# Graph attention on one core: a finer wait for the gathers, and two operands of VectorE kept in PSUM

## What is computed

```python
h  = (x @ W).reshape(n, HEADS, OUT_C)            # 8 heads of 32 channels
a1 = jnp.sum(h * attn_l, axis=-1); a2 = jnp.sum(h * attn_r, axis=-1)
e  = leaky_relu(a1[src] + a2[dst], 0.2)
ex = jnp.exp(e - seg_max[dst])
denom   = segment_sum(ex, dst)
message = h[src] * (ex / denom[dst])[:, :, None]
out     = segment_sum(message, dst)
```

## Time and profile before

| | |
|---|---|
| median of 3 runs | 3406.3 us (3402.91 to 3411.7) |
| span of the profiled execution | 3357.5 us (the rest of a run, some 49 us, lies around it) |
| busy: PE / DVE / ACT / POOL | 71% / 50% / 18% / 55% of the span |
| gathers on POOL | 1712, mean 1057 ns |
| DMA traffic | 302 MB, mean 90 GB/s |

### The profile page before, as it was taken

One profiled execution on the slowest core, in us unless ns is written; L12 is line 12 of the kernel. 1 busy time (PEld: TensorE's weight loads), 2 busy tenths in 40 slices (PEclk: granted clock), 3 DMA queues, 4 the chain that ended last, 5 costly groups with the idle time before them and its releaser, 6 DMA issues.

```text
span 3357.5 us, 47799 instructions
## 1 busy us (share of the span) xinstructions
PE 2396.9 (71%) x13450; PEld 1756.6 (52%) x13451; DVE 1666.8 (50%) x3416; ACT 614.4 (18%) x1640; POOL 1856.6 (55%) x1764
## 2 busy tenths in 40 slices
PE   4666776766677767666767666676778765379998
PEld 2554455545555555554545445554555554347776
DVE  6544445544445454544545445454555554733334
ACT  2411111111111111111111111011111111043332
POOL 3366666666666666666666666666666676200000
PEclk9878887878788777877878778888888887789999
DMA  6533333333333333333333333333334333100000
GB/s 193 200 99 88 89 96 93 96 97 92 91 96 93 92 97 92 89 94 92 91 97 96 93 91 101 100 99 96 109 106 109 109 94 84 39 29 19 19 19 20
DMA packets 150658, 302.18 MB, mean 90 GB/s; under 512 B 36163, under 2 KB 88347, under 8 KB 150620
## 3 DMA queue, kind: packets, MB, share of 16 engines
q0 software_dynamic: 82848, 233.35, 25.9%
q1 hardware_dynamic: 66100, 66.77, 6.1%
q10 hardware_dynamic: 1672, 1.59, 0.2%
HBM read 269.29 MB, written 32.29 MB: 90 GB/s over the span
## 4 chain that ended last, share of the span: by engine, by line
PE 43%; another core or an unknown queue 22%; DVE 16%; issue 12%; DVEq 2%; ACT 2%; POOL 2%; DMA 0%; ACTq 0%; SPq 0%; POOLq 0%
PE bank L872 16%; PE bank L985 5%; DVE work L1264 4%; PE bank L881 4%; PE bank L824 4%; PE bank L975 4%; DVE acc L1271 3%; PE bank L890 2%; PE bank L836 2%; PE bank L879 2%; POOL work L548 2%; PE bank L785 1%; DVEq L1256 1%; DVE zb L1245 1%
## 5 line engine op out<-in xcount | busy, mean ns | idle before, releaser
L548 POOL DMA_INDIRECT work<-h_tab,idx x1712 | 1809.5, 1057 | 949.9 <-issue 517.8
L872 PE MATMUL bank<-work 128*128 128x264 f32 x3424 | 1039.3, 452 | 420.1 <-DVE work L1264 293.0
L872 PEld LDWEIGHTS bank<-work 128*128 128x128 f32 x3424 | 717.2, 222 | 587.4 <-issue 366.7
L1271 DVE TENSOR_TENSOR acc<-bank,acc 128x264 f32 x856 | 369.0, 431 | 772.3 <-PE bank L872 313.0
L1264 DVE TENSOR_TENSOR work<-work 128x1024 f32<-128x1024 f32 x428 | 508.1, 1228 | 42.1 <-issue 33.9
L647 ACT CAST work<-bank 128x512 bf16<-128x512 f32 x428 | 237.7, 589 | 687.3 <-PE bank L824 427.4
L653 ACT ACTIVATE work<-zb 128x64 f32<-128x64 f32 x214 | 54.9, 256 | 1576.1 <-DVE zb L1249 1179.2
L1245 DVE TENSOR_TENSOR zb<-work,bank 128x64 f32<-128x64 f32 x214 | 47.0, 220 | 528.6 <-remote 489.5
L824 PEld LDWEIGHTS bank<-ident,work 128*128 128x128 f32 x1712 | 259.3, 172 | 92.2 <-issue 80.6
L824 PE MATMUL bank<-ident,work 128*128 128x128 f32 x1712 | 289.5, 321 | 20.9 <-issue 20.6
L836 PEld LDWEIGHTS bank<-a2p,work 128*128 128x128 bf16 x5136 | 203.5, 99 | 152.9 <-issue 114.3
(11 more groups left out here) (236 smaller groups left out, 1883.2 us busy)
## 6 DMA issues: line engine op xcount, KB each, us to landing
work<-h_tab,idx POOLq DMA_INDIRECT x1712
xx_d<-acc SPq DMA_DIRECT2D x49, 256.0 KB, 2.1
xnt_c<-xx_d SPq DMA_DIRECT2D x66, 128.0 KB
h_tab<-acc SPq DMA_DIRECT2D x49, 132.0 KB, 1.9
xn_c<-xx_d SPq DMA_DIRECT2D x49, 128.0 KB
q2t_d<-q2t_c SPq DMA_DIRECT2D x49, 128.0 KB
X<-x SPq DMA_DIRECT2D x6, 1024.0 KB, 11.7
out<-wqkv SPq DMA_DIRECT2D x16, 384.0 KB, 2.6
```

Source lines behind the costliest of these rows:

```text
L548: nc.gpsimd.indirect_dma_start(out=ring[q][:, j, :], out_offset=None, in_=h_tab, in_offset=bass.IndirectOffsetOnAxis(ap=idx[:, q, j:j + 1] ...
L872: ins = mm(bank[3 + s % 2][:, 0:TW], hot[q][:, s * G + g, :], ring[q][:, s * G + g, :], start=(g == 0), stop=(g == G - 1))
L1271: v.tensor_tensor(a, bank[3 + s % 2][:, 0:TW], a, ALU.add).then_inc(added, 1)
```

## The change

Three things:

1. POOL's wait goes from once per batch to once per two gathers: gathers 2k and 2k+1 of batch b wait until step k of batch b-3 is summed, in place of all four steps. The counter that it raises (`step_begun`) is raised four times a batch, not once.
2. ACT writes the exponentials twice: first into bank 2 of PSUM (`pk_ex`), which releases DVE, then into `ring[q]` as before, which releases PE's step 0 (`den_ready`). DVE's L1264 reads them from PSUM.
3. The row of node numbers is copied once into bank 2 of PSUM (`iota_b`), and the one-hots (L1162) read it from there. As the pick writes to the same bank, PE now waits ahead of the pick for batch b+1 until the one-hots of b+2 are made (`hot_ready`).

```diff
+        pk_ex = bank[2][:, TB * AW:TB * AW + TB * H].rearrange("p (j h) -> p j h", h=H)
+        iota_b = bank[2][:, 2 * P:3 * P]
@@ POOL
                 pool.wait_ge(idx_ready, b + 1)
-                wait(pool, summed, SB * (b - R3 + 1))
-                pool.sem_inc(batch_begun, 1)
                 for j in range(TB):
+                    if j % G == 0:
+                        wait(pool, summed, SB * (b - R3) + j // G + 1)
+                        pool.sem_inc(step_begun, 1)
                     nc.gpsimd.indirect_dma_start(
@@ ACT
-                nc.scalar.activation(ring[q][:, :, C:TW], zb[:, q, 0, :].rearrange("p (j h) -> p j h", h=H),
-                                     ACT.Exp).then_inc(ex_ready, 1)
+                u = zb[:, q, 0, :].rearrange("p (j h) -> p j h", h=H)
+                nc.scalar.activation(pk_ex, u, ACT.Exp).then_inc(ex_ready, 1)
+                nc.scalar.activation(ring[q][:, :, C:TW], u, ACT.Exp).then_inc(den_ready, 1)
@@ PE
+                    if s == 0:
+                        pe.wait_ge(den_ready, b + 1)
                     if s == 2 and not last:
+                        pe.wait_ge(hot_ready, b + 3)
                         pick(b + 1, (q + 1) % R3)
@@ DVE
-                v.tensor_tensor(hot[q], iota_p[:].unsqueeze(1).to_broadcast([P, TB, P]),
+                v.tensor_tensor(hot[q], iota_b.unsqueeze(1).to_broadcast([P, TB, P]),
+            own(v.tensor_copy(iota_b, iota_p[:]))
-                    ex = ring[q][:, k * 4:k * 4 + 4, C:TW].unsqueeze(3).to_broadcast([P, 4, H, HC])
+                    ex = pk_ex[:, k * 4:k * 4 + 4, :].unsqueeze(3).to_broadcast([P, 4, H, HC])
```

More of the change, by code:

```diff
@@ L306, in build @@
         idx_ready = sem("idx_ready")
-        batch_begun = sem("batch_begun")
+        step_begun = sem("step_begun")
         gathered = sems("gathered", R3)
@@ L315, in build @@
         ex_ready = sem("ex_ready")
+        den_ready = sem("den_ready")
         msg_ready = sem("msg_ready")
```

## The result

| | before | after |
|---|---|---|
| median, 4 runs each | 3404.6 us (3398.6 to 3411.7) | 3666.1 us (3660.0 to 3674.5) |
| span of the profiled execution | 3357.5 us | 3664.2 us |
| mean granted clock of TensorE in it | 0.833 | 0.788 |

The change makes the kernel slower, by a ratio of **1.077** (95% interval 1.0747 to 1.0798). The prediction was 3261 us with a range up to 3500: wrong in sign and outside the range. Its rival C stood at 3683 us.

What follows compares the result with a forecast made beforehand. The prediction took POOL to bound the kernel by a detour: its gather stream holds back PE's reports, then pauses. Freed gathers -183 and PE's wait +38 gave -145 us: 3406.3 - 145 = 3261 us, range 3090 to 3500.

Steps and rivals of the forecast that it cites:

- rival C: Slower: PE's wait for L1162 puts two reports in series, a second pause per batch; 14.2 us, 3683 us; chance 0.27.
- What bounds the kernel: Edge loop: POOL's gather stream holds back PE's reports, then pauses 2.0 us; together they set the 12.9 us batch.
- Operands in PSUM: L1264 and L1162 read one input from PSUM, so gathers lose 0.86 us of stretching per batch: -183 us.
- Speed with a PSUM input: DVE's operations take equally long with a PSUM input: price 0; the skill page's access cost would give 42 us.
- Second activation and copy: ACT's extra 0.256 us per batch is hidden behind L1264's first half, the node row copy is small: 0.
- PE's wait ahead of the pick: The pick starts after L1162, 1.1 us later, half paid in 69 prompt batches: +38 us, bounds 0 and +234.
- The wait per pair: POOL's looser waits lengthen some gather streams and cut others; counted as 0.
- A: Nothing gained: the pause grows from 2.0 to 2.9 us, taking back the freed gather time; 3406 us; chance 0.10.
- B: Longer gather streams: step reports come in while POOL runs, every second pause goes; 3050 us; chance 0.08.
- D: Gathers stay stretched, slowed by something else beside L1264; 3440 to 3640 us; chance 0.05.
- The last condition: If PE's late reports have another cause than POOL's stream, the prediction is wrong and L1162's wait is paid in full.

Runs made afterwards that it cites:

- e14: Kernel before, in effect unchanged (a meant second register load is not in the program), on a chip with late PE reports: ratio 1.004, 3358 us.
- e18: Kernel before with the exponentials in PSUM alone, on a chip with late PE reports: ratio 1.009 to the kernel before.
- e7: Kernel before, unchanged, on the chip with prompt PE reports: ratio 1.000.
- e9: Kernel before with the exponentials in PSUM alone, on the chip with prompt PE reports: ratio 0.965 to the kernel before.
- e3: Changed kernel with the node row back in SBUF and without PE's wait, on the chip with prompt PE reports: ratio 0.962 to the kernel before.
- e4: Kernel before with PE's wait for the one-hots alone, ahead of the pick's register load, on the chip with prompt PE reports: ratio 1.086.
- e10: Kernel before with PE's wait for the one-hots alone, behind the pick's register load, on the chip with prompt PE reports: ratio 1.006.
- e6: Changed kernel with PE's wait moved behind the pick's register load, on the chip with prompt PE reports: ratio 0.939 to the kernel before.
- e8: Changed kernel as it is, on the chip with prompt PE reports: ratio 1.050 to the kernel before.
- e15: Changed kernel as it is, on a chip with late PE reports: ratio 1.077 to the kernel before.
- e16: Changed kernel with PE's wait moved behind the pick's register load, on a chip with late PE reports: ratio 1.028 to the kernel before.
- e1: Kernel before with POOL's wait per pair of gathers alone, on the chip with prompt PE reports: ratio 1.000.
- e2: Changed kernel with POOL's wait put back to once per batch, on the chip with prompt PE reports: ratio 1.070 to the kernel before.
- e17: Changed kernel with the one-hots made ahead of step 0's add, on a chip with late PE reports: ratio 1.021 to the kernel before.
- e5: Changed kernel with the one-hots made ahead of step 0's add, on the chip with prompt PE reports: ratio 0.922 to the kernel before.

## Why the prediction was wrong

**What bounds the kernel: the pattern is there on the late chips, that POOL's stream sets the batch is not borne out.** Late reports and pauses come again in e14 to e18. But shorter gathers gave no shorter batch there (e18), and the chain of the profile had 2% POOL before, against 49% on the prompt chip (e7), where the kernel has no pause and POOL is the bound directly. What holds the reports back stays open; the same program has 498 us of such waits on one chip (e14) and none on another (e7).

**Operands in PSUM, -183 us: the gathers did what was said, the time did not.** Gather time fell by 186 us. This step failed where it took "a batch loses its 0.86 us" for "the batch gets shorter by 0.86 us". The prediction had the bound of zero, "if the pause takes its place", and took the other end, because the stretching lay beside just these operations. That is a reason for the gathers, not for the batch. e18 on the late chip: 111 us freed, 145 us more pause. On the prompt chip the step is right to 3 us for the part that e9 has (101 us of gathers, 104 us of time).

**Speed with a PSUM input: right.** L1273 takes 1.218 us and L1170 1.215 us, before 1.228 and 1.217. The access cost of the Trainium skill ("Perfetto Trace Analysis", Optimizing Scalar/DVE Operations) is not seen; the measurement decides.

**Second activation and copy, 0: nothing speaks against it.** In e9 and e3, which have the activation, the whole gain of the gathers arrives.

**PE's wait ahead of the pick, +38 us, at most +234: the step that decides the sign.** Alone it cost 0.086 x 2976 = 256 us on the prompt chip (e4), above the bound. Three things were left out. The price was taken from the end of the one-hots to the old start of the pick, 1.1 us, which by e10 costs next to nothing on that chip, and without what is queued behind the wait on PE: the register load, 0.70 us a batch, which makes the difference between 1.006 and 1.086. The pick was costed at the 0.75 us of the earlier trace rows; behind a wait it takes 1.70, as e6, e8 and the result show. The earlier trace rows had picks of 1.62 and 1.63 us before the prediction. And it was taken as a delay that lateness hides or that comes half back, not as a link that closes a circle. On the late chips no run has the wait alone; there the load's place is worth (1.077 - 1.028) x 3358 = 165 us (e15, e16).

**The sum against the result.** -145 us was forecast, +262 us measured, 407 us apart. The gain of 183 us that did not come and the 165 us of the load's place make 348 of them. The other 60 us, on top of the 38 us forecast for the wait, are not assigned.

**The wait per pair, 0: right where it could be tried.** 1.000 alone (e1); 2% in the change's favour beside a late PE (e2, e8). On the late chips open.

**Rivals.** C has the numbers that came: two pauses a batch, 14.3 us against its 14.2, 3666 us against its 3683, POOL idle 1432.4 / 214 = 6.7 us a batch (over 6), waits for the pick's report 918 us (over 600). Its mechanism is right only in that the pick hangs on step 0: e17 takes that away and falls from 1.077 to 1.021. Its condition, that step 0's own report is held back by the stream, did not come: waits for late reports ahead of the adds fell from 245.0 to 28.6 us. The long pause is PE's way from the pick through its queue to step 0. That 3683 lies so near is luck in part. A, the pause takes back what the gathers gave up, is what e18 measures on the late chip, a little worse than said (1.009 in place of 1.000). So the result is A's taking back of the gain and C's series without its late first report. B did not occur. D is out, the stretching is gone. The prediction argued against C with "a second pause gives a prompt pick"; in the rows of the result the pick behind the second pause is reported 2.3 us late (1233.04 to 1235.36), so that held for the step and not for the pick.

**The last condition**, that with another cause of the late reports the wait for L1162 is paid in full, was a rival in itself and got no chance. On the prompt chip, which has no late reports, the wait as built costs 256 us (e4); the delay by L1162 that it named costs 0.6% (e10).

## What to carry to other kernels

Where a wait goes into an in-order queue, price what stands between it and the instruction that needs it; a register load belongs ahead of the wait (1.086 against 1.006 here). Ask of each new wait whether it closes a circle through other engines: follow the result it waits for until it comes back to the waiter, and add up the links, the waiter's own queue among them. Here the freed engine shortened the period where it had no pauses (e9, 0.965) and not where it paused (e18, 1.009); where an engine pauses for reports, take the gain as open until a run shows it, and look at more than one chip before an 8% gain is believed.

## What the runs showed of the hardware

- The same kernel took 2968 to 2976 us on one chip and 3358 to 3405 us on others, 13 to 15% more. Gathers (0.949 us unstretched) and VectorE's operations (1.22 us) are equal. TensorE's reports are late while GpSimd issues gathers on the one kind (498 us of waits in e14) and prompt on the other (none in e7), and TensorE's same matmuls take longer (2398.8 us busy at a granted clock of 0.832 in e14, 2238.2 us at 0.884 in e7). Which of the two comes first is not shown.
- The edit that gains 7.8% on the one kind loses 2.1% on the other (e5, e17).
- Putting one operand of two in PSUM took 1.23 us operations out of the gathers' way: their mean is 1.082 us with three such operations a batch reading SBUF twice, 1.022 with one, 0.949 with none.
- The pick's 24 matmuls took 0.75 us or 1.62 us in the kernel before, both times close behind other matmuls and at a granted clock of 1.00; 158 of its 214 picks took under 1.2 us. In the kernels where they wait for one-hots made behind step 0's add (the result, e4, e6, e8, e10) each of the 214 took at least 1.62 us. So neither the clock nor idle time ahead of them explains it alone, and the profile doesn't show what does.
